# A fixed share of the lookups ahead of each gather: the score lookups of two attention layers

## The reference, cut to what matters

```python
def _gat_conv(h, src, dst, W, a_src, a_dst, bias):
    g = h @ W
    s = (g * a_src).sum(-1)
    d = (g * a_dst).sum(-1)
    e = jax.nn.leaky_relu(s[src] + d[dst], NEG_SLOPE)
    m = jax.ops.segment_max(e, dst, num_segments=N)
    ...
    ex = jnp.exp(e - m[dst])
    z = jax.ops.segment_sum(ex, dst, num_segments=N)
    alpha = ex / z[dst]
    out = jax.ops.segment_sum(g[src] * alpha[:, None], dst, num_segments=N)
    return out + bias
...
for l in range(L):
    h = _gat_conv(h, src_sl, dst_sl, lyr_W[l], att_src[l], att_dst[l], lyr_bias[l])
```

## Time and profile before

| | us |
|---|---|
| median of 3 runs | 7929.77 |
| the runs | 7909.9 to 7938.46 |
| span of the profiled execution | 7961.8 |
| busy in it: TensorE matmuls | 3988.6 (50%) |
| busy: VectorE | 3552.5 (45%) |
| busy: GpSimd | 4190.2 (53%) |
| busy: ScalarE | 1543.9 (19%) |

### The profile page before, as it was taken

How to read it: one execution, slowest core, us unless ns; L and a number is a source line. 1 busy time by engine, 2 the same in 40 slices (tenths; PEclk the granted TensorE clock), 3 DMA queues, 4 the chain that set the end, 5 groups by cost and what they waited for, 6 DMA issues and landing times. The chain is left out here.

```text
span 7961.8 us, 106930 instructions
## 1 busy us (share of the span) xinstructions
PE 3988.6 (50%) x29332; PEld 3225.4 (41%) x29332; DVE 3552.5 (45%) x10985; ACT 1543.9 (19%) x3920; POOL 4190.2 (53%) x4416
## 2 busy tenths in 40 slices
PE   2401645540164442334444458888888585333446
PEld 1301534530154432323444446666666473233334
DVE  3002965530297442423333355555555693122224
ACT  0001730010174000200000033444344213000003
POOL 6474035537503566466665635555555644666662
PEclk8655557775555766655555578888888797566568
DMA  5233445643344554345666424445444372111111
GB/s 147 75 105 96 146 125 171 188 117 106 94 145 131 161 168 140 108 104 141 149 150 147 109 87 143 147 149 149 145 147 145 79 206 64 46 46 45 45 45 32
DMA packets 564740, 944.43 MB, mean 119 GB/s; under 512 B 122022, under 2 KB 226111, under 8 KB 563599
## 3 DMA queue, kind: packets, MB, share of 16 engines
q1 hardware_dynamic: 263779, 403.40, 15.9%
q0 software_dynamic: 140576, 316.92, 15.5%
q10 hardware_dynamic: 159840, 217.27, 9.7%
HBM read 703.64 MB, written 235.53 MB: 118 GB/s over the span
## 5 line engine op out<-in xcount | busy, mean ns | idle before, releaser
L256 POOL DMA_INDIRECT s_rows<-rel_tab,src_v x832 | 813.4, 978 | 700.0 <-DVE s_msg L2489 424.7
L256 POOL DMA_INDIRECT stash<-gat_tab,src_g x784 | 790.9, 1009 | 724.5 <-POOLq L111 383.2
L256 POOL DMA_INDIRECT stash<-in_x,src_g x736 | 740.4, 1006 | 719.3 <-POOLq L111 382.6
L1163 PE MATMUL g_psc<-g_parts,g_oh 128*128 128x52 bf16 x9408 | 507.0, 220 | 1060.3 <-issue 796.5
L256 POOL DMA_INDIRECT gcn_rows<-gcn_tab,src_g x784 | 753.0, 960 | 461.8 <-issue 222.4
L256 POOL DMA_INDIRECT ggn_rows<-ggn_tab,src_g x784 | 744.2, 949 | 423.0 <-issue 231.0
L1600 PE MATMUL e_psb<-tmp,e_oh 128*128 x3328 | 565.5, 334 | 751.4 <-DVE e_oh L1571 470.4
L1163 PEld LDWEIGHTS g_psc<-g_parts,g_oh 128*128 128x128 bf16 x9408 | 439.7, 120 | 1128.2 <-issue 843.8
L1600 PEld LDWEIGHTS e_psb<-tmp,e_oh 128*128 128x128 f32 x3328 | 510.5, 237 | 806.7 <-issue 806.5
L1946 PE MATMUL ggn_pso<-ggn_rows,ggn_oh 128*128 x1952 | 448.7, 390 | 652.3 <-issue 277.2
L2116 PE MATMUL gcn_pso<-gcn_rows,gcn_oh 128*128 x1952 | 503.3, 433 | 531.4 <-issue 387.1
(11 more groups left out here) (503 smaller groups left out, 8232.0 us busy)
## 6 DMA issues: line engine op xcount, KB each, us to landing
edge_v<-stash SPq DMA_DIRECT2D x392, 256.0 KB, 2.1
g_lo_rows<-lo_rows ACTq DMA_DIRECT2D x392, 256.0 KB
e_values<-edge_v SPq DMA_DIRECT2D x392, 256.0 KB
oh_dram<-tmp ACTq DMA_DIRECT2D x208, 256.0 KB
s_oh<-oh_dram SPq DMA_DIRECT2D x208, 256.0 KB
edge_v<-acc SPq DMA_DIRECT2D x208, 256.0 KB
r_values<-edge_v SPq DMA_DIRECT2D x208, 256.0 KB, 3.0
tmp<-drel_rows ACTq DMA_DIRECT2D x208, 128.0 KB
```

Of the source, the lines that this page charges most:

```text
L256: pool.indirect_dma_start(rows[:, t, :], None, tab[:, :], bass.IndirectOffsetOnAxis(ap=edges[:, t:t + 1], axis=0)).then_inc(s_land, 16)
L1163: m = nc.tensor.matmul(ps_c[k % 2][:, a * GT + t, 0:NBP], oh[:, k, a * GE + t * P:a * GE + (t + 1) * P], part[:, a, n, :], start=(n == 0), ...
```

## The change

`keep_gathers` gets two more arguments: a semaphore and a function of the group's number. Where they are given, GpSimd waits ahead of group j until the semaphore has reached the function's value. Only the lookup stages give them: the semaphore is `s_c`, and for j from 3 on the value is 4 plus the whole part of (j - 2) x 196 / n, with n = 79 or 76 kept groups. So the first three groups go at once, the fourth waits for two finished lookups, the fifth for four, and so on evenly; the last waits for 188 of 196. The gathers themselves, their order, the stores and all other stages stay as they are.

```diff
-        def keep_gathers(pool, tab, first, n, s_land, s_st):
+        def keep_gathers(pool, tab, first, n, s_land, s_st, s_pace=None, pace=None):
 
             for j in range(n):
                 r, k = j // KEEP, j % KEEP
+                if s_pace is not None and pace(j) > 0:
+                    pool.wait_ge(s_pace, pace(j))
                 if r > 0:
                     pool.wait_ge(s_st[k], r * 16)
                 pool.sem_inc(s_turn, 1)
...
                 tabs = (dcol, scol)
+
+                def lookups(j):
+
+                    return RING + (j - 2) * GROUPS // (last - first) if j > 2 else 0
+
                 with nc.Block() as block:
...
-                        keep_gathers(pool, gat_src(l), first, last - first, k_land, k_st)
+                        keep_gathers(pool, gat_src(l), first, last - first, k_land, k_st, s_c, lookups)
```

## The result

The changed kernel takes 7489.02 us (median of 4 runs, 7487.12 to 7518.35) against 7934.11 us (4 runs, 7909.9 to 7955.14): a ratio of 0.9449, 95% interval 0.9432 to 0.9467. That is 445 us less; the forecast was 7455, in the range 7200 to 7660. The profiled execution has a span of 7486.0 us.

A forecast was written before the change was run, and what follows sets the result against it. The prediction took the lookup stages to last the sum of gathers and lookups; pacing saves 245 us in layer 0 and 233 in layer 1, 478 together, from 7961.8 to 7484, in median terms 7455 us, range 7200 to 7660.

The forecast's parts named there:

- Sum of both jobs: Lookup stages: gathers and lookups add up instead of overlapping, 789 us in layer 0 and 772 in layer 1.
- How the slowness comes: TensorE beside gathers: spaced matmuls begin 7.7 to 7.9 us into a run; full pace returns 2.3 us after a short run.
- What holds TensorE: Lookups beside gathers: not another engine's result, nor the clock; instructions 1.4 to 3.5 us apart, a signal 21 us late.
- The price of a group: Lookup stages: four kept gathers with their paced lookups cost 6.7 us in layer 0, 6.9 in layer 1.
- the last lookups: End of each lookup stage: 8 lookups remain after the last group is let go, 15 us.
- Gathers and VectorE: Whether a busy VectorE stretches gathers: 1026 ns beside working VectorE in layer 0's weighted sums, 985 with it idle.
- stretched gathers: Rival for the lookup stages: each one-hot blocks one gather, 7.8 us per group, about 7610 us; chance 0.14.
- Fully hidden: Rival for the lookup stages: TensorE never slows, 5.15 to 5.9 us per group, 7200 to 7310 us; chance 0.15.
- Slower: Rival for the lookup stages: every stop costs 27 us of drain, 19.3 us per group, 9390 us; chance 0.07.
- the 27 us drain: After layer 0's last gather, spaced matmuls go on and VectorE moves only 27 us later.
- The stated limit of 8.4 us: Drain per stop from which two groups take the 20 us they take now, so the change becomes slower.
- Nothing moves: Rival for the lookup stages: TensorE's loss is per gather and only spread out, 7903 us; chance 0.06.

The follow-up runs named there:

- long condition: Sets of runs in which the kernel before takes about 7934 us, as in the result; the changed kernel takes 7489.02 us there.
- short condition: Sets of runs in which the kernel before takes 5996 to 5998 us; the changed kernel, run again unaltered, takes 5995.81 us, ratio 1.0.

## Why the prediction was right

**Sum of both jobs.** Shown: with the two jobs forced one after the other the stages grow by 23 us of 1568. And the gain comes with the overlap: waits at every group and at every gather bring the two stages from 1568 to 1136 and 994 us. All of this holds for the long condition. That the trace read for the prediction was of that condition was luck: nothing in the prediction foresaw the other, in which the change gains nothing.

**How the slowness comes.** Single matmuls begin 7.9 us into the run of eight; 7.7 to 7.9 was read from the earlier trace rows. After the run's end VectorE moves at 420.89, 1.5 us later, where 2.3 was read from the earlier trace rows.

**What holds TensorE.** One reading of the earlier trace rows was wrong. The lookup that ends at 409.35 is the fourth, and the take at 430.36 is the third, by count and by the program's order; the third lookup's last matmul started at 342.8. So that signal was 88 us late and not 21. Nor is TensorE held by nothing but itself: within a lookup the program has no wait between matmuls, and there the prediction's reading stands, but the fourth lookup's first matmul (365.8) waits for the one-hot that VectorE makes at 365.44, after its late take at 363.86, and 23 of the 67 us per lookup are this wait:

```profile
363.86 0.59 DVE L1095 TENSOR_TENSOR g_eq<-g_eq,g_psc 128x416 f32<-128x416 f32 x1 [46.16 <-remote]
...
365.44 0.34 DVE L1082 TENSOR_SCALAR g_oh<-g_lo_rows,g_pid 128x512 bf16<-128x512 bf16 x1
```

The forecast didn't use the 21 us, so no number hangs on it.

**The price of a group, the term that was mis-sized.** 6.7 and 6.9 us were forecast, 529 and 524 us of gathers. Measured are 557 us (304.81 to 861.95) for 79 groups, 7.05 each, and 540 us for 76, 7.1 each. The step that failed is "the lookups released meanwhile are more than 2.48 if TensorE keeps pace, so GpSimd goes straight on to a second group". In layer 0, 36 runs of four gathers and 16 of eight ended in a stop (41 and 13 in layer 1). The run of four takes 6.71 us on average with a stop of 1.81: GpSimd goes on 2.7 us (median) after the last matmul of the lookup that its wait names, and 1.1 us after it where a stop of over 5 us has let the signals recover. The run of eight takes 15.45 us with a stop of 5.33, where 13.8 with 3.5 was forecast. Only 2.6 lookups are done in its first 7.8 us, not 4.3, because VectorE gets TensorE's signals late and makes the next one-hots late: signals sent during the run's first gather are taken after 0.87 us, during the second after 1.9, during the fourth after 7.3 (medians). That 6.7 us is also the length of the runs of four is luck: it was worked out for pairs of groups, and the pairs take 7.7 each. Of the 46 us between 478 forecast and 432 measured for the stages, 28 are layer 0's and 16 layer 1's gathers; the last lookups took 17.0 and 14.7 us, forecast 15.

**Gathers and VectorE.** The mean gather went from 988 ns (the prediction's 985 counts one more, short operation) to 997; not the 1.1 us that would have spoken for stretched gathers. The experiments say more, in the long condition both: with VectorE idle 1003 ns (308.85 over 308), with VectorE busy 382 of 505 us and a wait at every gather 971 ns. The Trainium skill (SBUF — State Buffer, "SBUF: two separate sides") has GpSimd shut out for as long as a VectorE operation in a two-port mode lasts, 620 ns becoming 3100; by the same section the pair of ports goes to whichever of the two starts first, and the other waits. No gather row shows the first. VectorE's one-hot does get longer beside gathers:

```profile
L1089 DVE TENSOR_SCALAR g_oh<-g_lo_rows,g_pid 128x512 bf16<-128x512 bf16 x190 | 76.3, 402 | 1.6 <-DMA g_lo_rows<-lo_rows 1.6
```

It takes 402 ns, 355 before, some 9 us over 190 of them, and 425 ns beside the unbroken gathers of the short condition (83.2 us over 196). That the port is the reason is not shown.

**The rivals.** Fully hidden (5.15 to 5.9 us per group) is false in the long condition, and nearly true in the short one at 4 x 1.273 = 5.1, where there is nothing to gain. Slower: the 27 us drain exists, but behind a long unbroken run only; a stop after four or eight gathers costs 1.8 or 5.3 us. The stated limit of 8.4 us was never reached. Nothing moves: true in the short condition, by another mechanism than the one given.

**What stays open.** What makes a stage slow beside gathers. It is not TensorE's clock (0.50 in both conditions), not TensorE's own queue alone (the drain without lookups), not the moving of the data (the drain without a packet), and not this kernel's code or the chip as such. Argued only: something on which instructions and semaphores of all engines depend together with GpSimd's gathers; the grid of 0.70 us and the missing updates point there. The recording of the events is an untested candidate, and so it is open too whether the long times and the 445 us exist in a run that nobody records. Why one set of runs has the slowness and the next on the same chip has not is open as well.

## What to carry to other kernels

Where two engines with no data in common are busy in turns, hold the one that disturbs with a counter of the other's progress, and in the smallest steps: four gathers per wait gained 5.5%, one per wait 7.4%. Run it in more than one set before believing the figure: here the whole gain exists only where the kernel before takes 7934 us, and where it takes 5996 the wait is free and useless. And before a trace's "issue" and "remote" are read, compare its count of semaphore updates with that of a quicker run of the same program. The better version for both is the wait ahead of each gather: 7351 us in the long condition and no different from the kernel before in the short one.

## What the runs showed of the hardware

The same program with the same granted clocks in its lookups takes 7489 us or 5996 us. In the long condition, beside gathers that follow each other freely, VectorE takes what TensorE signals after 1.7 to 1.9 us (the medians of the two paced kernels; 0.66 without gathers) and after up to 88 us deep in a run; late matmuls come at multiples of 0.70 us; after 316 gathers in a row even a stage change with no matmul pending takes 26.6 us instead of 5.7, and 21 semaphore clears of GpSimd in it 14.7 us instead of 1.3; and nine in ten of the semaphore updates by DMAs are missing from the trace there (704 of 6320). In the short condition a lookup beside an unbroken run takes 1.91 us against 1.83 alone.
